# Local attention's output: copied out of PSUM by ScalarE and scaled by GpSimd in place of one multiply on VectorE

## The reference

```python
def attn_layer(x, Wqkv, qs, ksc, Wo):        # 16 heads of 64, windows of 32
    q, k, v = ...                            # x @ Wqkv, split into heads
    q = l2norm(q) * qs; k = l2norm(k) * ksc  # then rotary embedding with scale
    out = local_attention(q, k, v)           # each window sees itself and the one before
    return out @ Wo

# in local_attention
sim = einsum('bhwie,bhwje->bhwij', bq, bk2) * 8.0      # masked
attn = softmax(sim, -1)
out = einsum('bhwij,bhwje->bhwie', attn, bv2)

def ffn_layer(x, g, bln, W1, b1, W2, b2):
    xn = layernorm(x) * g + bln
    a, gate = split(xn @ W1 + b1)
    return a * gelu(gate) @ W2 + b2

for i in range(6):
    x = attn_layer(shift_tokens(x), ...) + x
    x = ffn_layer(shift_tokens(x), ...) + x
```

## Time and profile before

| | |
|---|---|
| median of 3 runs | 4414.46 us (4410.03 to 4418.47) |
| profiled execution | 4412.12 us, span 4410.3 us |
| granted TensorE clock, mean | 0.959 |
| busy share PE / PEld / DVE / ACT / POOL | 85% / 65% / 81% / 60% / 66% |
| first and last instructions of the stack's units | about 896 and 4384 us |

### The profile page before, as it was taken

How to read it: one execution, slowest core, us unless ns; L and a number is a source line. 1 busy time by engine, 2 the same in 40 slices (tenths; PEclk the granted TensorE clock), 3 DMA queues, 4 the chain that set the end, 5 groups by cost and what they waited for, 6 DMA issues and landing times. The chain is left out here.

```text
span 4410.3 us, 109941 instructions
## 1 busy us (share of the span) xinstructions
PE 3768.9 (85%) x41516; PEld 2856.2 (65%) x41516; DVE 3571.7 (81%) x5298; ACT 2656.4 (60%) x4035; POOL 2895.4 (66%) x2520
## 2 busy tenths in 40 slices
PE   5666666669999899998999989999899999899996
PEld 3444444357777777776777767777677777677774
DVE  6777777678888788887888878888888888888884
ACT  5666666546666566656566656656566656566663
POOL 3555555357777677676767666777677676667672
PEclk9888888889999999999999999999999999999998
DMA  1111111032222322223222232222322222222221
GB/s 38 53 53 53 53 53 45 8 90 64 55 60 56 92 59 62 56 58 91 62 55 62 56 88 65 55 58 54 89 60 67 56 56 78 70 60 63 56 55 58
DMA packets 157205, 267.21 MB, mean 61 GB/s; under 512 B 32062, under 2 KB 51644, under 8 KB 152380
## 3 DMA queue, kind: packets, MB, share of 16 engines
q1 hardware_dynamic: 157116, 266.19, 22.1%
HBM read 44.81 MB, written 26.21 MB: 16 GB/s over the span
## 5 line engine op out<-in xcount | busy, mean ns | idle before, releaser
L789 POOL TENSOR_TENSOR st_qk_rot<-st_qk_rot,st_qk_sq 128x1024 f32<-128x1024 f32 x384 | 920.4, 2397 | 939.6 <-DVE st_qk_sq L686 939.6
L429 PE MATMUL st_ps<-st_wqkv,st_xs 128*128 128x512 f32 x3456 | 956.7, 412 | 66.2 <-DMA st_wqkv<-wqkv_parts 37.7
L537 ACT ACTIVATE st_qk_sq<-st_ps 128x1024 f32<-128x1024 f32 x384 | 393.9, 1026 | 652.6 <-PE st_ps L429 652.0
L429 PEld LDWEIGHTS st_ps<-st_wqkv,st_xs 128*128 128x128 f32 x3456 | 612.4, 190 | 231.4 <-issue 97.8
L809 POOL TENSOR_TENSOR st_qk_rot<-st_qk_rot,st_rn 128x1024 f32<-128x1024 f32 x384 | 722.7, 1903 | 15.0
L1426 POOL TENSOR_TENSOR at_probs<-at_probs,at_rden 128x128 f32<-128x128 f32 (+3 forms) x512 | 361.8, 738 | 389.6 <-DVE at_rden L1357 389.6
L668 DVE TENSOR_REDUCE st_nt<-st_qk_sq 128x16 f32<-128x1024 f32 x384 | 465.7, 1213 | 175.5 <-ACT st_qk_sq L537 175.4
L686 DVE TENSOR_TENSOR st_qk_sq<-st_ps,st_rot 128x512 f32<-128x512 f32 x768 | 490.2, 678 | 0.0
L672 DVE TENSOR_TENSOR st_qk_rot<-st_ps,st_rot 128x1024 f32<-128x1024 f32 x384 | 465.9, 1213 | 8.6 <-PE st_ps L444 8.6
L444 PE MATMUL st_ps<-consts_sb,st_qk_rot 128*128 128x128 f32 x3072 | 403.0, 274 | 27.9 <-DVE st_hid L769 16.5
L437 PEld LDWEIGHTS st_ps<-st_oT,st_wo 128*128 128x128 f32 x3072 | 368.8, 192 | 79.4 <-issue 75.8
(11 more groups left out here) (125 smaller groups left out, 6828.4 us busy)
## 6 DMA issues: line engine op xcount, KB each, us to landing
st_v_bd<-st_v_tok SPq DMA_DIRECT2D x1152, 128.0 KB, 2.3
st_v_bd<-st_v_tok SPq DMA_DIRECT2D x672, 64.0 KB, 2.1
wqkv_parts<-at_w_parts SPq DMA_DIRECT2D x18, 1024.0 KB, 4.5
st_wqkv<-wqkv_parts SPq DMA_DIRECT2D x18, 1024.0 KB, 5.7
at_w_raw<-in_wqkv SPq DMA_DIRECT2D x18, 512.0 KB, 4.1
rotary_tables<-at_rot SPq DMA_DIRECT2D x6, 512.0 KB, 2.8
st_rot<-rotary_tables SPq DMA_DIRECT2D x24, 128.0 KB, 2.4
st_wo<-in_wo SPq DMA_DIRECT2D x6, 512.0 KB, 4.2
```

The lines of the kernel that those rows point to most:

```text
L429: last = pe.matmul(out[:, c * 512:(c + 1) * 512], xs[:, x_part, t * P:(t + 1) * P], rhs, start=(n == 0), stop=(n == len(PASSES) - 1))
L537: act.activation(qk_sq[:, cols_of(a)], slot_of("qk"[a], 0, t), ACT.Square).then_inc(squared[a], 1)
L789: pool.tensor_tensor(qk_rot[:, cols], qk_rot[:, cols], qk_sq[:, cols], ALU.add).then_inc(rot_done[a], 1)
```

## The change

VectorE's multiply (L759) is taken out. In its place:

- ScalarE copies o from PSUM to `st_o` one step later, as the first thing in its step, and posts `taken["o"]`.
- GpSimd multiplies `st_o` in place by the reciprocal of the sums, in the same step as the copy, ahead of its rotations and, in t = 1, behind the LayerNorm chain. It posts a new semaphore, `o_scaled`.
- TensorE's ot waits for `o_scaled` in place of `taken["o"]`.
- VectorE waits, before it sums the exponentials of a tile, for `o_scaled` of the tile two before, since that one's reciprocal lies in the same buffer.
- Each engine's loop can be preceded by filler, increments of a semaphore that nobody waits for. ScalarE gets 114 of them ahead of unit 0 of the stack; all others get none, and the first attention (`AT_FILL`) none.

```diff
+AT_FILL = {}
+ST_FILL = {"act": 114}
+
+def fill_block(eng, filled, n):
+    for _ in range(n):
+        eng.sem_inc(filled, 1)
...
-        def loop(eng, unit):
+        def loop(eng, unit, fill=0):
+            fill_block(eng, filled, fill)
             unit(0)
...
                             elif kind == "ot":
-                                pe.wait_ge(taken["o"], tiles_done(u, d, index))
+                                pe.wait_ge(o_scaled, tiles_done(u, d, index))
...
@@ scalar
+                        if alive(u, d3):
+                            act.wait_ge(ready["o"], 2 + (n - 3))
+                            if not (start and n < 5):
+                                act.wait_ge(ready["ot"], n - 4)
+                            act.activation(o[:, :], slot_of("o", d2, t2), ACT.Copy).then_inc(taken["o"], 1)
                         if alive(u, 0):
                             square(0)
...
-                loop(act, unit)
+                loop(act, unit, ST_FILL.get('act', 0))
...
@@ vector
                             dve.wait_ge(exp_ready, n - 2)
+                            if not (start and n < 5):
+                                dve.wait_ge(o_scaled, n - 4)
                             dve.tensor_reduce(den[:, t2 % 2, 0, :], s[:, t2 % 2, :].rearrange("p (h k) -> p h k", h=HEADS),
                                               AX.X, ALU.add).then_inc(den_ready, 1)
                             dve.wait_ge(den_ready, 2 * (n - 2) - 1)
                             dve.reciprocal(den[:, t2 % 2, 1, :], den[:, t2 % 2, 0, :]).then_inc(den_ready, 1)
-                        if alive(u, d2):
-                            dve.wait_ge(ready["o"], n)
-                            dve.wait_ge(den_ready, 2 * (n - 2))
-                            if not (start and n < 4):
-                                dve.wait_ge(ready["ot"], n - 3)
-                            dve.tensor_tensor(
-                                o[:, :].rearrange("p (h d) -> p h d", h=HEADS),
-                                slot_of("o", d2, t2).rearrange("p (h d) -> p h d", h=HEADS),
-                                den[:, t2 % 2, 1, :].unsqueeze(2).to_broadcast([P, HEADS, DH]),
-                                ALU.mult).then_inc(taken["o"], 1)
...
@@ gpsimd
+                        d, tt = divmod(t - 3, TILES)
+                        if alive(u, d):
+                            pool.wait_ge(taken["o"], n - 3)
+                            pool.wait_ge(den_ready, 2 * (n - 3))
+                            by_head = o[:, :].rearrange("p (h d) -> p h d", h=HEADS)
+                            pool.tensor_tensor(by_head, by_head, den[:, tt % 2, 1, :].unsqueeze(2).to_broadcast([P, HEADS, DH]),
+                                               ALU.mult).then_inc(o_scaled, 1)
```

More of the change, by code:

```diff
@@ L220, in local_stack @@
         ps = ctx.enter_context(nc.psum_tensor("st_ps", [P, NBANKS * BANK], F32))
+        filled = sem("filled")
         small_in, wo_in, w12_in = sem("small_in"), sem("wo_in"), sem("w12_in")
@@ L243, in local_stack @@
         ff_gain, ff_newton, pool_own = sem("ff_gain"), sem("ff_newton"), sem("pool_own")
+        o_scaled = sem("o_scaled")
         def jobs_of(t):
@@ L504, in unit @@
                             last.then_inc(ready[kind], 1)
-                loop(pe, unit)
+                loop(pe, unit, ST_FILL.get('pe', 0))
             @block.scalar
@@ L771, in unit @@
                                                          ALU.add, ALU.mult).then_inc(taken["h"], 1)
-                loop(dve, unit)
+                loop(dve, unit, ST_FILL.get('dve', 0))
             @block.gpsimd
@@ L838, in unit @@
                                                ALU.subtract).then_inc(shifted, 1)
-                loop(pool, unit)
+                loop(pool, unit, ST_FILL.get('pool', 0))
 AH = 16
@@ L966, in jobs_at, with loop @@
                     if (step, p) == (s % AH, part) and (not kinds or kind in kinds)]
-        def loop(eng, batch):
+        def loop(eng, batch, fill=0):
+            fill_block(eng, filled, fill)
             batch(-1)
@@ L1140, in batch @@
                         m_products(b, s, 1)
-                loop(pe, batch)
+                loop(pe, batch, AT_FILL.get('pe', 0))
             @block.scalar
@@ L1216, in batch @@
                                     take(b, job)
-                loop(act, batch)
+                loop(act, batch, AT_FILL.get('act', 0))
             @block.vector
@@ L1383, in batch @@
                             finish_norm(b, -1, True)
-                loop(dve, batch)
+                loop(dve, batch, AT_FILL.get('dve', 0))
             @block.gpsimd
@@ L1428, in batch @@
                         last.then_inc(weights_ready, 1)
-                loop(pool, batch)
+                loop(pool, batch, AT_FILL.get('pool', 0))
 def last_residual(nc, const_sb, mod, xT, x1_dram, out):
```

## The result

| | before | after |
|---|---|---|
| median | 4413.16 us (4 runs, 4410.03 to 4418.47) | 4707.11 us (4 runs, 4706.14 to 4711.11) |
| ratio after / before | | 1.0666 (95% interval 1.0648 to 1.0685) |
| span of the profiled execution | 4410.3 us | 4705.7 us |
| granted TensorE clock, mean | 0.959 | 0.935 |

A forecast was written before the change was run, and what follows sets the result against it. TensorE was taken to set the pace. 46 units x (3.0 + 0.6 + 1.5) = 235 us, filler 3 and 5 behind the loop, on 4412.1, gave 4655, or 4657 as the runs' median; range 4575 to 4722.

The forecast's parts named there:

- wait in t = 1, without the clock: In t = 1 ot starts 3.2 us later, behind GpSimd's LayerNorm chain and multiply; cost 2.8 to 3.2, taken as 3.0.
- t = 2: In t = 2 ScalarE's copy has no cover and delays square of k and the exponential pt awaits: 0.6 us a unit.
- clock: TensorE's 4.9 us idle before ot lowers its clock, slowing ot and pt: 1.5 us a unit, bounds 0 to 2.9.
- 46 units: The loop's units, each longer by 3.0 + 0.6 + 1.5 us: 235 us in all.
- filler: ScalarE's 114 increments run once ahead of its first unit: 0 to 6.5 us, taken as 3.
- behind the loop: The last three tiles pass an uncovered chain after the loop, each 1.7 us longer: 5 us.
- from there the gelu and t = 2 follow h, so nothing gives them back: After ot's delay in t = 1, the 3.0 us left at the feed-forward's h matmuls are not recovered later.
- the upper bound of 2.9 taken from the warm-up: Most the clock's fall could cost a unit: half of the 5.9 us of slow work seen in the warm-up.
- No clock loss (4588): Rival: same wait in each unit but no fall of TensorE's clock, 174 us, 4588 us; chance 0.15.
- Faster by VectorE's relief (4359): Rival: in t = 1 ot starts 1.2 us earlier without VectorE's multiply, 55 us gained, 4359 us; chance 0.04.
- Balance: Rival: GpSimd's delay and VectorE's relief cancel, time within 0.2% of before; chance 0.03.
- Code fetched in every unit by ScalarE (4781): Rival: filler fails and ScalarE's longer loop fetches code each unit, 2.7 us (0 to 5.4), 4781 us; chance 0.06.

The follow-up runs named there:

- the early copy alone: Changed kernel, with ScalarE's copy of o for t = 2 done at the end of t = 1, ahead of the gelus; 4654.24 us, ratio 1.0551.
- the kernel with two dummies: Changed kernel plus two unused 128x512 matmuls on TensorE ahead of its wait for the scaled o in t = 1; 4690.29 us, ratio 1.0639.
- two more places mended: Multiply-ahead kernel plus ScalarE's earlier copy for t = 2 and the norm's last step moved from VectorE to ScalarE; 4384.93 us, ratio 0.9948.

## Why the prediction was right, and where it was short

| term | predicted | measured |
|---|---|---|
| wait in t = 1, without the clock | 3.0 us a unit | 3.7 (3.3 at ot; at h 0.63 in place of 0.24, so 0.4) |
| t = 2 | 0.6 | 0.6 |
| clock | 1.5 | 0.8 in 15 units, 2.7 in 25 |
| 46 units | 235 us | 283 (276 + 6.8) |
| filler | 3 us | 4.04 at its place, nothing measurable in the whole |
| behind the loop | 5 us | 15.5 |

**The mechanism is the one forecast.** GpSimd's LayerNorm chain stands ahead of the multiply, ot waits 5.0 us for it in each unit (4.9 was forecast) but those behind a weight load, where it waits 3.2 to 3.5, VectorE's 227 us are not on the path, and t = 3 and t = 0 are as before. Putting the multiply ahead of the chain takes 229 us back. ScalarE's copy costs 0.6 us in t = 2 by the changed kernel's own windows and by the early copy alone.

**The wait was mis-sized by 0.7 us.** The forecast let 0.2 us of the 3.2 go, because h had waited 0.24 us in the earlier trace rows. The kernel with two dummies shows that ot comes 3.3 us later and that h then waits 0.63 us where the forecast had none left. The step that failed is "from there the gelu and t = 2 follow h, so nothing gives them back", which took for granted that h's input stays ready. It comes from VectorE's L756. Before (L736 there), it started at 2555.90 beside GpSimd's small [128 x 32] instruction of 0.47 us (2556.01). In the kernel with two dummies it starts at 2671.93 beside the scalings of q and k, of some 1.9 us each:

```profile
2555.90 0.48 DVE L736 TENSOR_SCALAR st_xc<-st_xc,st_ln_b 128x512 f32<-128x512 f32 x1
2671.47 3.94 POOL L824 TENSOR_TENSOR st_qk_rot<-st_qk_rot,st_rn 128x1024 f32<-128x1024 f32 x2
```

This could have been asked of the trace of before. There a small [128 x 32] instruction on VectorE (L679) takes 1.56 us and ends at 2552.40, with GpSimd's L789 that ends at 2552.37, while the same instruction (L699) took 0.17 us in the kernel with the multiply ahead of the chain. Before, then with the multiply ahead:

```profile
2550.84 1.56 DVE L679 TENSOR_SCALAR st_ss<-st_nt 128x32 f32<-128x32 f32 x1
2728.39 0.17 DVE L699 TENSOR_SCALAR st_ss<-st_nt 128x32 f32<-128x32 f32 x1
```

**The clock was mis-sized both ways.** ot and pt ran slower by 0.88 and 0.67 us in the short unit, as the earlier trace rows had it (1.5). But part of that time h would have waited for L756 anyway, so the net is 0.8. In the long units the lower level reaches on into sim (3.10 in place of 1.95), and the net is 2.7, near the upper bound of 2.9 taken from the warm-up. The mean net is about (15 x 0.8 + 25 x 2.7) / 40 = 2.0. That the clock falls in every unit, as the Trainium skill has it (TensorE: Matmul & The Clock Gate, "HAM oscillation — how this bites in real kernels"), agrees with the trace: ot takes 1.94 us in t = 1 of 44 of the loop's 45 units and 1.78 in its first. What decides between a short and a long stretch at the lower level stays open; the waits of 5.02 and 5.03 us don't tell them apart. But it isn't chance: the order is regular, and with a unit 0.6 us shorter, in the early copy alone, two of three units are short instead of one. So this part of the loss can move with small changes of a unit's length, and a price of the clock that is read from one kernel need not hold for the next.

**The drain was mis-sized most, for its length.** The forecast counted the two new instructions for three tiles, 5 us. It left out what stands ahead of them in program order, and the drain grew by 15.5. The last two ot, then ScalarE and GpSimd for the last:

```profile
4624.34 1.94 PE L491 MATMUL st_ps<-consts_sb,st_o 128*128 128x128 f32 x8 [7.01 <-POOL st_o L842]
...
4645.01 1.94 PE L491 MATMUL st_ps<-consts_sb,st_o 128*128 128x128 f32 x8 [5.18 <-POOL st_o L842]
```

```profile
4641.86 1.02 ACT L571 ACTIVATE st_o<-st_ps 128x1024 f32<-128x1024 f32 x1
```

```profile
4642.96 1.90 POOL L842 TENSOR_TENSOR st_o<-st_o,st_den 128x1024 f32<-128x1024 f32 x1 [18.77 <-ACT st_o L571]
```

The first waits for the multiply behind the last LayerNorm chain. The second's o was in PSUM by 4634.48 (o matmuls 4632.52 + 1.96), but the copy is the first thing of the step behind the last gelus and runs at 4641.86; GpSimd had nothing to do for 18.8 us. The early copy alone takes 8.7 us of it back.

**The rivals.** No clock loss (4588) is out: the clock falls, though 4.3 of the 5.1 us of a short unit are not the clock's. Faster by VectorE's relief (4359) is no mishap of the reasoning: with the multiply ahead of the chain, ot does come 1.3 us earlier. In the change as made it can't, since GpSimd's chain ends too late, and even then VectorE's last step of the norm has to be out of GpSimd's way before it shows in the time. Balance is out. Code fetched in every unit by ScalarE (4781) is out both with and without the filler; the middle of its bounds is not tested by these runs, but what it costs on TensorE is: about 4 us of issue at each jump.

## What to carry to other kernels

Before an operation goes to an engine with time to spare, look at what stands ahead of it in that engine's order at the one moment where the bound engine needs it: here the same multiply costs 6.7% behind four instructions, and with it ahead of them, and two more places mended, the kernel is 0.5% faster than before. A wait of the bound engine costs more than its length if its clock falls with it, so price a wait by the work behind it as well. And when a long instruction moves on GpSimd, look again at the length of VectorE's instructions that will run beside it, in particular those that feed the bound engine.

## What the runs showed of the hardware that I had not expected

- One VectorE multiply-add [128 x 512] in SBUF took 0.48 us in the kernel before, 0.75 and 1.72 and 2.50 us in others, and each time that it was long it ended 0.28 or 0.29 us behind GpSimd's instruction beside it.
- TensorE's loop, held without fetches in the changed kernel, fetched its code in six units with two dummy matmuls more in it and in each unit with three or more: 9 packets, 0.15 MB and some 4 us of issue a pass, and the matmuls behind it at the lower clock. 60 increments ahead of the loop did not help.
- After equal waits of 5.0 us the lower clock lasted for ot and pt in 15 units and into sim in 25, in a regular order; with a unit 0.6 us shorter it was 28 and 12.
- The attention stage ahead of the stack, unchanged in every kernel, ended up to 21 us apart between profiled executions (at 872.8 and 893.7 us), so the unit's length decides here more sharply than one execution's total.
